# State space runs on one core: the input turned in the run ahead, the input projection resident, conv taps read from PSUM, softplus by channel block, scans begun at two blocks, gate products inside the scan loop

## The reference

```
xn = x * rsqrt(mean(x*x) + 1e-5) * w_norm          # _rmsnorm of the layernormed input
xz = xn @ W_in                                     # 256 -> 1024
xs, res = split(xz, 2)
xs = silu(depthwise_causal_conv(xs, conv_w) + conv_b)      # 4 taps
A = -exp(A_log)
xdbc = xs @ W_xp                                   # 512 -> 128 (dt_r) + 16 (B) + 16 (C)
delta = softplus(dt_r @ W_dt + b_dt)
h_t = h_(t-1) * exp(delta_t * A) + delta_t * B_t * u_t     # per channel and state, u = xs
y_t = sum over states of h_t * C_t,  then + u * D
out = (y * silu(res)) @ W_out + x
```

## Time and profile before

| | |
|---|---|
| time, median of 3 runs | 1806.8 us (1806.35 to 1812.46) |
| the profiled execution's own time | 1820.19 us |
| its span | 1818.4 us |
| PE busy | 1584.0 us, 87% of the span |
| DVE busy | 1232.2 us, 68% |
| ACT busy | 932.5 us, 51% |
| POOL busy | 691.9 us, 38% |
| first `state_space` block | 732.5 to 927.9 us |
| second `state_space` block | 927.9 to 1122.9 us |

### The profile page before, as it was taken

How to read it: one execution, slowest core, us unless ns; L and a number is a source line. 1 busy time by engine, 2 the same in 40 slices (tenths; PEclk the granted TensorE clock), 3 DMA queues, 4 the chain that set the end, 5 groups by cost and what they waited for, 6 DMA issues and landing times. The chain is left out here.

```text
span 1818.4 us, 26103 instructions
## 1 busy us (share of the span) xinstructions
PE 1584.0 (87%) x8448; PEld 1231.3 (68%) x8448; DVE 1232.2 (68%) x2586; ACT 932.5 (51%) x1973; POOL 691.9 (38%) x624
## 2 busy tenths in 40 slices
PE   6998778979998898867876887888999898999899
PEld 4776678957776888333533444667888686788787
DVE  6888747658777777599968996444666534666643
ACT  5555446746655565554435543225565444566543
POOL 5999932333222231075715765002222232222222
PEclk9999979989999999988998998998999898999999
DMA  3221032111113120100010000002112111111111
GB/s 121 73 81 63 22 114 77 44 51 35 45 45 102 59 87 4 49 1 1 0 49 1 0 1 6 6 3 66 35 44 75 36 69 56 33 46 46 64 58 47
DMA packets 29704, 82.46 MB, mean 45 GB/s; under 512 B 6052, under 2 KB 10920, under 8 KB 27320
## 3 DMA queue, kind: packets, MB, share of 16 engines
q1 hardware_dynamic: 28440, 75.10, 12.6%
q0 software_dynamic: 1184, 6.37, 1.0%
HBM read 80.40 MB, written 1.05 MB: 45 GB/s over the span
## 5 line engine op out<-in xcount | busy, mean ns | idle before, releaser
L815 POOL TENSOR_TENSOR head_low<-head,head_high 128x512 fp32r<-128x512 f32 x64 | 81.9, 1280 | 460.5 <-ACT head_high L805 459.7
L2174 POOL TENSOR_TENSOR rings<-xp,Bs 128x512 f32<-128x512 f32 x128 | 193.7, 1515 | 163.0 <-DVE state L2113 82.8
L1714 POOL TENSOR_TENSOR experts_low<-experts,experts_high 128x1536 fp32r<-128x1536 f32 (+1 forms) x64 | 144.3, 2258 | 286.3 <-ACT experts_high L1660 163.6
L1167 ACT ACTIVATE probs<-banks,neg_max 128x512 f32<-128x512 f32 (+3 forms) x256 | 131.7, 527 | 152.0 <-DVE neg_max L1077 152.0
L1962 PE MATMUL banks<-rings,ident 128*128 128x512 f32 x256 | 140.3, 648 | 66.1 <-DVE rings L2142 66.1
L2113 DVE TENSOR_TENSOR_SCAN state<-banks,rings 128x512 f32<-128x512 f32 x128 | 155.4, 1215 | 0.0
L2048 ACT ACTIVATE banks<-delta,A 128x512 f32<-128x512 f32 x128 | 88.4, 692 | 119.2 <-DVE state L2113 108.3
L201 PE MATMUL banks<-experts_high,xnT_high 128*128 128x384 f32 (+1 forms) x384 | 141.5, 368 | 6.7 <-POOL experts_low L1714 6.7
L1411 DVE SCALAR_TENSOR_TENSOR hidden<-banks,weight,act_out 128x96 f32<-128x96 f32 (+1 forms) x192 | 62.7, 368 | 117.4 <-ACT act_out L1379 117.2
L201 PE MATMUL banks<-experts_low,xnT_high 128*128 128x384 f32 (+1 forms) x384 | 139.5, 363 | 0.0
L201 PE MATMUL banks<-experts_high,xnT_low 128*128 128x384 f32 (+1 forms) x384 | 139.1, 362 | 0.0
(11 more groups left out here) (281 smaller groups left out, 4761.3 us busy)
## 6 DMA issues: line engine op xcount, KB each, us to landing
head<-in_heads SPq DMA_DIRECT2D x64, 384.0 KB, 3.1
experts<-in_experts SPq DMA_DIRECT2D x16, 1152.0 KB, 5.2
experts<-in_experts SPq DMA_DIRECT2D x16, 768.0 KB, 4.3
values<-in_values SPq DMA_DIRECT2D x32, 256.0 KB, 3.2
coef<-in_spline_coef POOLq DMA_DIRECT2D x8, 768.0 KB, 4.6
idx<-in_lut_idx SPq DMA_DIRECT2D x16, 134.0 KB, 2.1
Cs<-in_w_in SPq DMA_DIRECT2D x2, 1024.0 KB, 4.8
x<-in_x SPq DMA_DIRECT2D x2, 512.0 KB, 4.6
```

What stands on the lines that cost most here:

```text
L1167: last = nc.scalar.activation(prob_tile(i), score_tile(i), ACT.Exp, bias=neg_max[:, i:i + 1], scale=QK_SCALE, accum_out=row_sum[:, i:i + 1])
L1714: nc.gpsimd.tensor_tensor(parts[gpar][1][:, columns], raw[gpar][:, columns], parts[gpar][0][:, columns].bitcast(FP32), ALU.subtract)\
L2174: nc.gpsimd.tensor_tensor(inflow[:, step % INFLOWS], du[:, c], Bs[:, n], ALU.mult)\
```

## The change

In one go:

- `w_in` (1 MB in SBUF) is a tensor held over layer 0 and layer 1. It is loaded once, by SP in the layer 0 block of sequence 1, after the last query and key of that block (`projection_ahead`). In layer 0 the rope tables and `rot` lie in its first 64 partitions (`lend_rope`). The high and low parts of `xnT` of sequence 1 are now given back during layer 1 (`hold_parts`).
- The rms scaling and second transposition of the input move into the block ahead: `Norm` for layer 1 has 11 phases in place of 8, with `add_input` (POOL, `x += xn`), `scale_again` (DVE), `turn_again` (PE) and `store_again` (ACT). For it the mixture's unrolled tail grows from 8 to 16 items.
- The four x blocks are projected into four banks with no wait between them. The conv reads its taps from PSUM; the copy into `xp` is gone.
- `to_bc` goes ahead of `to_rank`. `FIRST` falls from 8 rows to 3, and `LEAD` = 6 rows are spread before the loop.
- Softplus goes block by block. ACT makes Abs, Exp and Ln of blocks 0 and 1, DVE their Relu, sum and product; the scans begin then. Abs and Relu, Exp and Ln of blocks 2 and 3 are hung on ACT's steps 0 to 7, their sums and products on POOL's steps 10, 14, 18 and 22.
- The z products are in the loop (PE steps 28, 31, 35, 38). For z 0 and 1 ACT makes a Tanh and DVE two multiplications in place of ACT's Silu.
- The 16 MLP items are 3 or 4 steps apart, from step 7 to step 61. ACT's Tanh stands ahead of the row copy in its step. The Norm of the other sequence starts at step 37 in place of 32.

```diff
+    def hold_projection(self, stage_ctx):
+        sb = self.local(stage_ctx)
+        self.w_in = sb("w_in", [P, KD, 2 * CH])
+        self.xmT = [sb("xmT", [P, T])[:], self.xn[:, 0:2].rearrange("p t d -> p (t d)")]
...
+    def add_input(self, pool):
+        pool.wait_ge(self.normed.sem, self.normed.at(NT))
+        self.m.nc.gpsimd.tensor_tensor(self.x[:], self.x[:], self.m.xn[:], ALU.add).then_inc(self.added.sem, 1)
+    def scale_again(self, dve):
+        dve.wait_ge(self.turned.sem, self.turned.at(KD))
+        dve.wait_ge(self.added.sem, self.added.at(1))
+        for t in range(NT):
+            xn = self.m.xn[:, t]
+            self.m.nc.vector.tensor_scalar(xn, xn, self.rms[:, t:t + 1], None, ALU.mult).then_inc(self.scaled.sem, 1)
...
-    SPREADS, FIRST = 2 * NS, 8
-    BEHIND = 4
+    SPREADS, FIRST, LEAD = 2 * NS, 3, 6
-    item_at = lambda step, after: (step - after) // PER if step >= after and (step - after) % PER == 0 else None
-    TANH, GATE, ADD = 3, 1, 2
+    GATE_AT = {7 + i * 54 // (ITEMS - 1): i for i in range(ITEMS)}
+    ADD_AT = {step + 1: i for step, i in GATE_AT.items()}
+    TANH_AT = {step + 2: i for step, i in GATE_AT.items()}
+    MULTIPLY_FIRST = 3
+    ABS_AT, RELU_AT = {0: 3, 2: 2}, {0: 3, 3: 2}
+    EXP_AT, LN_AT, TABLE_AT = {4: 2, 5: 3}, {6: 2, 7: 3}, 8
+    DELTA_ADD, DELTA_TIMES = {10: 2, 18: 3}, {14: 2, 22: 3}
+    Z_AT = {28: 0, 31: 1, 35: 2, 38: 3}
+    Z_BEND = {31: 0, 34: 1, 38: 2, 41: 3}
+    Z_GATE = {30: 0, 33: 1}
+    Y_GATE = {35: 0, 36: 1}
...
+        NORM_LOW, NORM_ADD = {}, 46
+        XM_TURN, XM_STORE = {49: 0, 53: 1}, {52: 0, 56: 1}
...
+    x_psum = lambda c: bank((4, 5, 2, 3)[c])
...
     def take_x(c):
             act.wait_ge(x_projected.sem, x_projected.at(c + 1))
-            nc.scalar.activation(xp[:, c, TAPS - 1:], projected_psum(c), ACT.Copy).then_inc(xs_ready.sem, 1)
-            act.wait_ge(xs_ready.sem, xs_ready.at(c + 1))
-            nc.scalar.activation(conv[:, c], xp[:, c, 0:T], ACT.Identity, scale=vec[:, c, 0:1], bias=vec[:, c, 4:5])\
-              .then_inc(first_tap.sem, 1)
+            nc.scalar.activation(conv[:, c], x_psum(c), ACT.Identity, scale=vec[:, c, TAPS - 1:TAPS],
+                                 bias=vec[:, c, 4:5]).then_inc(first_tap.sem, 1)
...
+                last = nc.vector.scalar_tensor_tensor(conv[:, c, back:], x_psum(c)[:, 0:T - back], vec[:, c, j:j + 1],
+                                                      conv[:, c, back:], ALU.mult, ALU.add)
...
+        store_first(0)
+        relu_dt(0)
+        finish_delta(0)
+        store_first(1)
+        relu_dt(1)
+        finish_delta(1)
+        store_first(2)
         dve.sem_inc(scanned.sem, DECAYS)
...
+            if step in DELTA_ADD:
+                late = DELTA_ADD[step]
+                pool.wait_ge(logged.sem, logged.at(late + 1))
+                pool.wait_ge(dt_taken.sem, dt_taken.at(2))
+                nc.gpsimd.tensor_tensor(delta[:, late], delta[:, late], du[:, late], ALU.add)\
+                  .then_inc(delta_ready.sem, 1)
+            if step in DELTA_TIMES:
+                late = DELTA_TIMES[step]
+                pool.wait_ge(delta_ready.sem, delta_ready.at(late + 1))
+                nc.gpsimd.tensor_tensor(du[:, late], delta[:, late], u[:, late], ALU.mult)\
+                  .then_inc(du_ready.sem, 1)
...
+def projection_ahead(m):
...
+    def sync(sp):
+        sp.wait_ge(turned.sem, turned.at(HEADS))
+        sp.dma_start(m.w_in[:], m.dram["w_in"]).then_inc(loaded.sem, 16)
```

More of the change, by code:

```diff
@@ L110, in __init__ @@
         self.xnT_of = [sb(f"xnT{b}", [P, KD, T]) for b in range(BATCH)]
[L111 to L112 removed]
+        self.xnT_parts_of = [[sb(f"xnT_{part}0", [P, KD, T], FP32R) for part in ("high", "low")], None]
         self.rms_of = [sb(f"rms{b}", [P, NT]) for b in range(BATCH)]
@@ L643, in vector @@
             self.low(dve, 1)
+        if phase == 6 and self.with_xm:
+            self.scale_again(dve)
     def scalar(self, act, phase):
@@ L2015, in scalar, with relu_dt, exp_dt @@
-        for c in range(KC):
-            take_x(c)
-        for c in range(KC):
-            silu_u(c)
+            nc.scalar.activation(du[:, c], dt_psum(c), ACT.Abs, bias=vec[:, c, 5:6]).then_inc(softplus_step.sem, 1)
+        def relu_dt(c):
+            nc.scalar.activation(delta[:, c], dt_psum(c), ACT.Relu, bias=vec[:, c, 5:6]).then_inc(dt_taken.sem, 1)
+        def exp_dt(c, step):
+            act.wait_ge(softplus_step.sem, softplus_step.at(step))
+            nc.scalar.activation(du[:, c], du[:, c], ACT.Exp, scale=-1.0).then_inc(softplus_step.sem, 1)
@@ new lines, in ln_dt @@
+        def ln_dt(c, step):
+            act.wait_ge(softplus_step.sem, softplus_step.at(step))
+            nc.scalar.activation(du[:, c], du[:, c], ACT.Ln, bias=1.0).then_inc(logged.sem, 1)
+        act.wait_ge(vec_loaded.sem, vec_loaded.at(16))
+        take_x(0)
+        take_x(1)
+        silu_u(0)
+        take_x(2)
+        silu_u(1)
+        take_x(3)
+        silu_u(2)
+        silu_u(3)
+        nc.scalar.preload_act_table_set("natural_log_exp_and_others")
+        act.wait_ge(loaded.sem, loaded.at(16 * len(loads)))
@@ L2031, in scalar @@
[L2031 to L2040 removed]
+        for c in range(2):
+            abs_dt(c)
+            exp_dt(c, 2 * c + 1)
+            ln_dt(c, 2 * c + 2)
@@ L2143, in vector @@
               .then_inc(product_ready.sem, 1)
-            item = item_at(step, GATE)
-            if item is not None:
+            if step in GATE_AT:
+                item = GATE_AT[step]
                 dve.wait_ge(bent.sem, bent.at(item + 1))
@@ L2392, in attention_layer @@
     first, heads = attention(m, layer, ctx, ahead=ahead, buffers=buffers)
-    run(m, first, *before, heads, experts, join(m, b, done, out=out))
+    run(m, first, *before, heads, experts, *after, join(m, b, done, out=out))
 def hybrid_stack_kernel(nc, dram, out):
@@ L2410, in hybrid_stack_kernel @@
-        with ExitStack() as layer_ctx:
-            attention_layer(m, 1, 0, layer_ctx, Norm(m, 0, 1, (5, 5)), GROUPS, (powers(m, layer_ctx),))
-        for b in range(BATCH):
-            with ExitStack() as layer_ctx:
-                m.turn_to(b)
-                xn_added = m.sig("xn_added")
-                norm = Norm(m, 1 - b, 1 + b, (2, 2), (xn_added.sem, xn_added.at(1)))
-                scan, done = state_space(m, b, layer_ctx, norm)
-                run(m, scan, join(m, b, done, (xn_added, 1)))
@@ L2419, in hybrid_stack_kernel @@
-        with ExitStack() as parts_ctx:
-            parts = [parts_ctx.enter_context(nc.sbuf_tensor(f"lut_{part}", [P, LUT_COLS], FP32R))
-                     for part in ("high", "low")]
+        with ExitStack() as projection_ctx:
+            m.hold_projection(projection_ctx)
+            with ExitStack() as parts_ctx:
+                m.hold_parts(parts_ctx)
+                with ExitStack() as rows_ctx:
+                    spline = SplineRows(m, rows_ctx)
+                    with ExitStack() as layer_ctx:
+                        m.turn_to(0)
+                        constants, decay = transition(m, layer_ctx)
+                        first, heads = attention(m, 0, layer_ctx, spline, norm_here=True)
+                        split_weights, first.scalar = first.scalar, None
+                        run(m, constants, first, Norm(m, 0, 0, (0, 1)).stage(split_weights), decay, heads)
+                    with ExitStack() as layer_ctx:
+                        experts, _, done = mixture(m, 0, layer_ctx, 0, rows=spline.turn_beside(5),
+                                                   norm=Norm(m, 1, 0, (5, 5)))
+                        run(m, experts, join(m, 0, done))
+                with ExitStack() as layer_ctx:
+                    attention_layer(m, 1, 0, layer_ctx, Norm(m, 0, 1, (5, 5)), GROUPS, (powers(m, layer_ctx),),
+                                    (projection_ahead(m),))
```

390 lines of the change are left out of this document (217 added, 173 removed).

## The result

The changed kernel takes 1792.5 us in the median of 4 runs (1791.6 to 1795.4), the kernel before 1809.1 in the median of 4 (1806.4 to 1812.5; the three known before the change, and one more). The ratio is 0.991, with a 95% interval from 0.989 to 0.993: faster, by 16.6 us where 36.2 were forecast, and above the range of 1756 to 1788. The profiled execution of the changed kernel took 1795.4 us by its own time, 2.9 above the median; that of before was 11 us above its median, so stages are compared here and not the two spans.

A forecast was written before the change was run, and what follows sets the result against it. Prelude bound by an engine-to-engine chain, loop by DVE. Preludes -45.1, loops +4.9 and +1.5, mixture +2.5 sum to -36.2 us; from 1806.8 that gives 1770.6, with an 8-in-10 range of 1756 to 1788.

The forecast's parts named there:

- The prelude (-45.1): Both block preludes: shorter engine-to-engine chain, from 47.8 and 47.3 us to 25 each, together -45.1 us.
- rival C: Projections: PE granted the low clock (0.50) again, +6.9 us a block, kernel at 1784; chance 0.10.
- Tanh ahead of the row copy (-6.9): ACT in the loop: Tanh no longer stands behind the row copy, so 6.9 us of DVE waits go.
- Three-step distances (+4.9): MLP items in the loop: three steps (5.2 us) fall short of 6.3, costing 1.1 or 0.9 each, +4.9 us.
- the term of -2.0: DVE's Tanh waits in each loop: 6.9 us removed and 4.9 added back, net -2.0 us.
- POOL's four sums and products ... I cost at nothing ... may be four inflows ahead: Loop, blocks 2 and 3: at least 1.09 us each on POOL, costed at nothing; uncovered, 1.1 to 1.6 each.
- The price of a blocked product, 0.45 us: Loop: one wait of DVE's product for POOL costs 0.45 us, from `u * silu_z` at 1.136 against 0.69.
- Rival E: Loop: POOL could go first in every step and DVE's product wait, 57 us over 128 steps, 1828; chance 0.06.
- POOL's addition (+2.0): First block's loop, step 46: POOL's `x += xn` holds up a DVE product, +2.0 us, between 0 and 2.34.
- ACT's first steps (+1.6): ACT's first eight loop steps: softplus instructions and a table load just ahead of the first Tanh, +1.6 us.
- rival D: ACT crowded in its first eight loop steps: upper bound 6.9 us, +5.3 a block, kernel 1781; chance 0.12.
- The mixture (+2.5): Mixture ahead: its tail gains `scale_again`, transposes, copies and POOL's addition, nothing to 4.6 us, middle +2.5 taken.

The follow-up runs named there:

- the execution without a slow multiply: Changed kernel with rows copied four steps ahead, plus Norm's second store on ACT moved behind Tanh (step 51 to 52): 1777.6 us, ratio 0.982.

## Why the prediction was right and wrong

- **The prelude (-45.1): right.** 25.0 and 25.3 us against 25, so -44.8. The projections ran at the full clock, which rules out rival C; the first Abs came at 17.7 against 17.4; the conv was hidden.
- **Tanh ahead of the row copy (-6.9): right**, shown alone in the kernel before, -7 us a loop.
- **Three-step distances (+4.9): right in size.** In the execution without a slow multiply the waits are 5.5 and 4.9 us, of which 0.8 is the first gate's, single ones 1.0 and 0.8, and step 35 is the covered one (0.26). What was left out is the item that comes late for another reason: in the changed kernel one gate of 3.92 us in the first loop, and 1.84, 1.96 and 3.21 in the second, together about 3 and 6 us more than distance gives. The 1.96 is Norm's store ahead of Tanh, at a distance of four. So the term of -2.0 came out at +1.1 and +4.1. In the kernel before no gate waited over 1.86 us, and multiplies of 2.40 and 2.21 us were each followed by a wait of 0.76.
- **"POOL's four sums and products ... I cost at nothing ... may be four inflows ahead": this step failed**, though not by those instructions, which moved to DVE changed little but their own cost. Its cover was what wasn't there. The text took the ring of four inflows for POOL's slack and did not ask what else an inflow needs: its row, which ACT now copied two steps ahead in place of four. The move of that copy is in the diff and stood in no term. It cost 5.4 and 4.4 us of product time (two steps against four), of 9.2 and 7.1.
- **The price of a blocked product, 0.45 us: wrong by more than half.** It was taken from a multiplication whose mean is 1.136. A product that POOL has got well ahead of takes 1.5 to 1.7 us, 0.8 to 1.0 more. Rival E had the mechanism (POOL goes first) and a wrong shape: not every step, but 9 to 13 of 64.
- **POOL's addition (+2.0):** 1.3 us in the loop. **`scale_again` (+1.4):** 2.2; of its four instructions one took 1.37 us, behind an inflow of POOL, and the others 0.34 (the mean of 598 ns hides this). **z gates (+1.4):** 1.4 for the gates themselves; the products of steps 32 and 33, in no term, took 1.3 us more. **ACT's root (+0.5):** nothing waited for it in either loop.
- **ACT's first steps (+1.6):** 0.5 us of scans waiting in each loop, 0.45 us ahead of the first gate, and 0.7 for the first product, behind PE's spreads. Together 1.65, which is in part luck, since the 0.7 is not ACT's; rival D's 6.9 is refuted.
- **The mixture (+2.5):** the layer with the longer tail was 2.1 us shorter in the profiled execution. No cost is seen, but the stages behind the two blocks, which the change does not touch, were 4.2 us shorter too (691.1 in place of 695.3), so a cost of a microsecond or two would not be seen.
- **The sum.** 28.1 us of growth in the loops where 6.4 were forecast makes 21.7; the mixture gives 4.6 back. -36.2 + 21.7 - 4.6 is -19.1, and the medians say -16.6.

On the blocked products the Trainium skill ("SBUF — State Buffer", section "Who interferes with whom") says that the order of issue decides who blocks. The runs agree: the product at 809.39 is 0.11 us behind POOL's inflow and takes 1.70 us, and the scans, one of whose two inputs lies in PSUM, keep 1.21 to 1.22 us in all kernels. The prediction quoted this rule and left the order to "POOL's waits on the scans". That was true of the kernel before, and the change had made it untrue.

What stays open is what lets PE's clock fall in the middle of one loop and not of the other. The rest of the product time with rows four steps ahead (46.6 against 42.8 us in the first loop) is in a few products: the first (1.61 us, 0.85 before), step 15 (1.07, behind POOL's product for block 2), steps 32 and 33 (1.34 each, around the z and y gates; which of these lets POOL go first there was not tried), and steps 43 and 44 with POOL's addition.

## What to carry to other kernels

Where instructions of two engines block each other, the order in which they start is part of the schedule: for each instruction on the one ask what event lets it go, before and after the change, and whether that is still the event which also lets the other go first. A ring's depth is not slack by itself; slack is the least of all lookaheads that an instruction needs, and a constant that quietly goes from four to two can take it away. And where a change brings much in one place, run its smallest part alone: here the order of two instructions on ACT brought 15 us by itself, the whole change 17.

## What was not expected of the hardware

- DVE sums and products of two SBUF inputs, 0.67 to 0.69 us alone, took up to 1.76 us beside POOL; one `tensor_scalar` on 256 columns took 1.37 us behind an inflow, and its three neighbours 0.34.
- The granted clock can fall by half in the middle of a loop in which PE is 80% busy: a multiply of 1.89 us took 2.84 and 3.15 in the changed kernel. Behind the same idle time of 2.7 us PE came back at the full clock in one loop and at the low one in the other, and filling the idle time with eight products of one row did not prevent the fall (3.06 us).
